# A decoder layer with attention, retention and a two-expert feed-forward: the experts' rows are added to one row per token in memory, the last norm loads all tokens at once, and the down products go chunk by chunk

## What is computed

```python
x = _layernorm(x + attention(x, Wq, Wk, Wv, Wo, bo))   # 16 heads of width 8, over the other rows of a token group
x = _layernorm(x + retention(x, ctx, ctx))             # decaying causal scores against ctx
router = x @ gate                                      # 8 experts, the best two per token, softmax over the two
hid = silu(x @ w1[e]) * (x @ w3[e])                    # 128 -> 512
x = _layernorm(x + sum over the two e of weight[e] * (hid @ w2[e]))
```

## Time and profile before

| | |
|---|---|
| device time, median of 3 runs | 1015.67 us (1014.71 to 1018.06) |
| profiled execution, first to last instruction (span) | 1027.0 us |
| PE busy, share of the span | 839.8 us, 82% |
| DVE | 794.7 us, 77% |
| POOL | 654.8 us, 64% |
| ACT | 607.7 us, 59% |
| mean granted TensorE clock | 0.914 of full speed |
| DMA | 72.72 MB, 71 GB/s over the span |

### The profile page before, as it was taken

The page is one execution under the profiler, slowest core; times in us unless marked ns, Lnnn a source line. Parts: engine busy times, 40 slices in busy tenths (PEclk is TensorE's granted clock), DMA queues, the critical chain, the costliest instruction groups (busy, mean ns, idle before and its releaser), DMA issues.

```text
span 1027.0 us, 35115 instructions
## 1 busy us (share of the span) xinstructions
PE 839.8 (82%) x12164; PEld 639.6 (62%) x12164; DVE 794.7 (77%) x2219; ACT 607.7 (59%) x1416; POOL 654.8 (64%) x738
## 2 busy tenths in 40 slices
PE   1667699999999999989979770699999999999600
PEld 1445466666666666656655440599899999999500
DVE  4787899998988989878856642588888888888575
ACT  1123457667667777666766851466666666666355
POOL 0338776699989999988997456044444444444443
PEclk9687899999999999999998965799999999999855
DMA  9312122122232231212222002222222222222186
GB/s 307 79 27 48 35 52 54 36 66 67 47 72 52 65 68 50 65 37 60 47 50 63 23 22 63 66 64 61 61 63 65 65 62 64 63 61 59 45 257 222
DMA packets 145303, 72.72 MB, mean 71 GB/s; under 512 B 75024, under 2 KB 134544, under 8 KB 145136
## 3 DMA queue, kind: packets, MB, share of 16 engines
q1 hardware_dynamic: 124800, 40.56, 17.1%
q0 software_dynamic: 8640, 17.84, 5.2%
q10 hardware_dynamic: 11696, 12.08, 3.6%
HBM read 42.11 MB, written 28.34 MB: 69 GB/s over the span
## 4 chain that ended last, share of the span: by engine, by line
PE 33%; POOL 28%; issue 11%; DVE 3%; DMA 2%; another core or an unknown queue 1%; ACT 1%; POOLq 0%; SPq 0%; DVEq 0%; ACTq 0%
POOL prod_ev L1551 14%; POOL routed_rows L1568 9%; PE QKV L773 9%; PE ST L773 9%; PE XT L801 5%; PE SC L801 5%; POOL rs L1531 3%; DMA prod_ev<-token_halves 1%; DMA routed_rows<-xe,pos 1%; PE YY L589 1%; POOL frs L1613 1%; PE YY L791 1%; PE TR L791 1%; PE SC L562 1%
## 5 line engine op out<-in xcount | busy, mean ns | idle before, releaser
L1551 POOL TENSOR_TENSOR prod_ev<-e_sb,q_v 128x512 f32<-128x512 f32 x256 | 300.3, 1206 | 77.5 <-PE YY L589 40.1
L1600 POOL DMA_INDIRECT token_halves<-w_new,tok_i x142 | 137.9, 971 | 32.5 <-issue 22.2
L1568 POOL DMA_INDIRECT routed_rows<-xe,pos x128 | 131.2, 1025 | 30.4 <-issue 30.0
L1151 DVE TENSOR_TENSOR prod_qk<-q_v,QKV 128x2048 f32<-128x2048 f32 x64 | 145.4, 2274 | 4.9 <-ACT q_v L870 4.9
L1453 DVE TENSOR_TENSOR prod_ev<-prod_qk,prod_ev 128x1024 f16<-128x1024 f32 x71 | 87.0, 1225 | 56.1 <-ACT prod_ev L1028 31.1
L773 PE MATMUL QKV<-k_t,w_hl 128*128 128x256 f16 x852 | 117.2, 274 | 0.0
L773 PE MATMUL ST<-k_t,w_hl 128*128 128x256 f16 x852 | 116.9, 274 | 0.0
L411 POOL TENSOR_TENSOR marks<-half_c 128x1 f32<-128x1 f32 x103 | 19.7, 192 | 149.7 <-DVE w_new L1469 149.1
L1037 ACT ACTIVATE prod_qk<-QKV,silu_scale 128x512 f32<-128x512 f32 x142 | 90.0, 683 | 41.3 <-PE QKV L773 41.3
L1028 ACT CAST prod_ev<-prod_qk 128x1024 f16<-128x1024 f32 x71 | 74.2, 1045 | 62.9 <-DVE prod_qk L1479 62.9
L1479 DVE SCALAR_TENSOR_TENSOR prod_qk<-ST,hid_scale,prod_qk 128x512 f32<-128x512 f32 x142 | 99.5, 742 | 2.9 <-PE ST L773 1.8
(11 more groups left out here) (171 smaller groups left out, 1785.9 us busy)
## 6 DMA issues: line engine op xcount, KB each, us to landing
w_new<-routed_rows SPq DMA_DIRECT2D x71, 130.0 KB
prod_ev<-token_halves SPq DMA_DIRECT2D x16, 512.0 KB, 4.9
x_sb<-x SPq DMA_DIRECT2D x32, 128.0 KB, 2.8
x_res<-x SPq DMA_DIRECT2D x128, 32.0 KB
head_rows<-o_n SPq DMA_DIRECT2D x32, 128.0 KB
o_t<-head_rows SPq DMA_DIRECT2D x64, 64.0 KB
ctx_sb<-ctx SPq DMA_DIRECT2D x32, 128.0 KB
out<-prod_qk ACTq DMA_DIRECT2D x16, 256.0 KB, 4.0
```

The source lines that it names most:

```text
L1151: eng.tensor_tensor(prod_qk[:, u, :, :].rearrange("p d (i j) -> p d i j", j=NH), q.unsqueeze(3).to_broadcast([P, HD, NH, NH]), k.unsqueeze ...
L1551: ins = eng.tensor_tensor(prod_ev[:, u, q, :, :, 0:HD], e_sb[:, it.slot(2), u, 64 * q:64 * q + 64].rearrange("p (i j) -> p j i", j=4).unsq ...
L1568: eng.indirect_dma_start(out=xs, out_offset=bass.IndirectOffsetOnAxis(ap=pos[:, r, 2 * u + k:2 * u + k + 1], axis=0), in_=xe[:, r, u, k, : ...
L1600: eng.indirect_dma_start(out=halves, out_offset=bass.IndirectOffsetOnAxis(ap=tok_i[:, s, u:u + 1], axis=0), in_=yw[:, s, u, :], in_offset= ...
```

## The change

Stage A also writes the normed x of each token, once, to a new tensor `token_sums` with one row per token: four direct DMAs a duo on SP's queue, behind the loads of `o_t` (`ROWS_LAG`). The row numbers behind the routed rows now name tokens, not halves. In stage B, `xh` and its half of x are gone, `yw` is the weighted product alone (`tensor_scalar`), and the indirect DMAs add their rows to `token_sums` (`compute_op`); since two tiles can hold the same token, POOL waits before each tile until the DMAs of the tile before have landed. The down products keep their matmuls and change their order. In stage C eight loads of 512 KB bring all sums at once into the memory of the weights `w1_hl` and `w3_hl`; there is no add of halves, ACT writes in place, and SP issues the stores. `C_FIRST` equals the number of chunks, so the stage is written out without a loop.

```diff
-        "spare_ids": 2 * n_tok + p[:, None] + P * np.arange(4 * n_exp)[None, :],
-        "ids": 2 * (P * b + row)[:, None] + 4 * P * (ids // 4) + 2 * S * (ids // 2 % 2) + ids % 2,
+        "spare_ids": n_tok + p[:, None] + P * np.arange(4 * n_exp)[None, :],
+        "ids": (P * b + row)[:, None] + 2 * P * (ids // 4) + S * (ids // 2 % 2),
...
-    PE_LAGS, ACT_LAGS, DVE_LAGS, POOL_LAGS, SP_LAGS = 13, 13, 14, 11, 9
-    CTX_LAG, HEADS_LAG = 9, 8
+    PE_LAGS, ACT_LAGS, DVE_LAGS, POOL_LAGS, SP_LAGS = 13, 13, 14, 11, 14
+    CTX_LAG, HEADS_LAG, ROWS_LAG = 9, 8, 14
...
-    C_FIRST, C_LAGS = 8, 3
+    C_FIRST, C_LAGS = n_chunks_c, 3
...
-    halves = nc.dram_tensor("token_halves", [2 * n_tok + 2 * n_exp * TILE, P], F32).ap()
+    sums = nc.dram_tensor("token_sums", [n_tok + 2 * n_exp * TILE, P], F32).ap()
...
-    half_rows = halves[0:2 * n_tok, :].rearrange("(p n k) d -> p n k d", p=P, k=2)
+    sum_duos = sums[0:n_tok, :].rearrange("(n u b h g) d -> n u b g h d", u=2, b=2, h=NH, g=4)
+    sum_rows = sums[0:n_tok, :].rearrange("(p n) d -> p n d", p=P)
...
-        fin = stage_b2[:, 0:RING * C_SLICES * 2 * P].rearrange("p (r n k d) -> p r n k d", r=RING, n=C_SLICES, k=2)
-        fout = stage_b[:, 0:RING * C_SLICES * P].rearrange("p (r n d) -> p r n d", r=RING, n=C_SLICES)
+        in_weights = [w[:, :, :].rearrange("p k w -> p (k w)").bitcast(F32).rearrange("p (c n d) -> p c n d", n=C_SLICES, d=P)
+                      for w in (w1_hl, w3_hl)]
+
+        def final_rows(c):
+
+            n = c.number()
+            return in_weights[n * 2 // n_chunks_c][:, n % (n_chunks_c // 2), :, :]
...
+                if it := at(ROWS_LAG):
+
+                    r = it.slot(RING)
+                    wait(it, x2_ready)
+                    for u in range(2):
+                        for b in range(2):
+                            eng.dma_start(sum_duos[it.number()][u][b], xe[S * u:S * u + S, r, b, 0, 0:P]).then_inc(rows_out[r], 16)
...
-                    wait(t, xh_ready, RING)
...
-
-                    wait(c, fout_ready, RING)
-                    eng.dma_start(fin[:, c.slot(RING), :, :, :],
-                                  half_rows[:, bass.ds(c.number() * C_SLICES, C_SLICES), :, :]).then_inc(fin_in[c.slot(RING)], 16)
-
-            run_steps(eng, n_chunks_c, C_FIRST, 0, last_norm)
+                    n, m = c.number(), n_chunks_c // 4
+                    eng.dma_start(in_weights[n // m][:, 2 * (n % m):2 * (n % m) + 2, :, :],
+                                  sum_rows[:, 2 * C_SLICES * n:2 * C_SLICES * (n + 1), :].rearrange("p (c n) d -> p c n d", c=2)
+                                  ).then_inc(fin_in[n], 16)
+
+            run_steps(eng, n_chunks_c // 2, C_FIRST // 2, 0, last_norm)
+
+            def store(at):
+                if c := at(0):
+                    wait(c, fout_ready)
+                    eng.dma_start(out_rows[:, bass.ds(c.number() * C_SLICES, C_SLICES), :], final_rows(c)).then_inc(fin_out, 16)
+
+            run_steps(eng, n_chunks_c, C_FIRST, 0, store)
+            eng.wait_ge(fin_out, 16 * n_chunks_c)
...
-                    for u in range(2):
-                        for n in range(n_chunk):
-                            cols = bass.ds(down_no * inner + P * n, P)
-                            for k, (h, wp) in enumerate(((hid_hi, 0), (hid_lo, 0), (hid_hi, 1))):
-                                mm = eng.matmul(YB[down.slot(2)][:, P * u:P * u + P],
-                                                h[:, down.slot(2), TILE * n + P * u:TILE * n + P * u + P], w2_hl[:, wp, cols],
-                                                start=(n == 0 and k == 0), stop=(n == n_chunk - 1 and k == 2))
+                    for n in range(n_chunk):
+                        cols = bass.ds(down_no * inner + P * n, P)
+                        for wp, terms in ((0, (hid_hi, hid_lo)), (1, (hid_hi,))):
+                            for u in range(2):
+                                for h in terms:
+                                    mm = eng.matmul(YB[down.slot(2)][:, P * u:P * u + P],
+                                                    h[:, down.slot(2), TILE * n + P * u:TILE * n + P * u + P], w2_hl[:, wp, cols],
+                                                    start=(n == 0 and wp == 0 and u == 0 and h is hid_hi),
+                                                    stop=(n == n_chunk - 1 and wp == 1), skip_group_check=True)
...
+                wait_ring(it, rows_out, RING, 64)
...
-                    wait_ring(t, xg_in)
-                    wait(t, yw_ready, RING)
-                    eng.mul(xh[:, t.slot(RING), :, :], xg[:, t.slot(RING), :, 0:P], 0.5).then_inc(xh_ready, 1)
...
-                    s, r = c.slot(2), c.slot(RING)
+                    y = final_rows(c)
                     wait(c, fnb_ready)
-                    wait_ring(c, fin_out, RING)
                     for n in range(C_SLICES):
-                        ins = eng.activation(fout[:, r, n, :], fin[:, r, n, 0, :], ACT.Identity,
-                                             bias=fnb[:, s, n:n + 1], scale=frs[:, s, n:n + 1])
+                        ins = eng.activation(y[:, n, :], y[:, n, :], ACT.Identity,
+                                             bias=fnb[:, c.slot(2), n:n + 1], scale=frs[:, c.slot(2), n:n + 1])
                     ins.then_inc(fout_ready, 1)
-                if c := at(3):
-                    wait(c, fout_ready)
-                    eng.dma_start(out_rows[:, bass.ds(c.number() * C_SLICES, C_SLICES), :],
-                                  fout[:, c.slot(RING), :, :]).then_inc(fin_out[c.slot(RING)], 16)
 
             run_steps(eng, n_chunks_c, C_FIRST, C_LAGS, last_norm)
...
-                    wait(t, xh_ready)
                     wait(t, wt_ready)
                     wait_ring(t, half_out, RING, 32)
                     for u in range(2):
-                        ins = eng.scalar_tensor_tensor(out=yw[:, s, u, :], in0=YB[t.slot(2)][:, P * u:P * u + P],
-                                                       scalar=wt[:, s, u:u + 1], in1=xh[:, s, u, :], op0=ALU.mult, op1=ALU.add)
+                        ins = eng.tensor_scalar(yw[:, s, u, :], YB[t.slot(2)][:, P * u:P * u + P], wt[:, s, u:u + 1], None, ALU.mult)
...
-                    y = fin[:, c.slot(RING), :, :, :]
-                    wait_ring(c, fin_in)
-                    eng.tensor_tensor(y[:, :, 0, :], y[:, :, 0, :], y[:, :, 1, :], ALU.add).then_inc(fsum_ready, 1)
-                    wait(c, fsum_ready)
+                    eng.wait_ge(fin_in[c.number() // 2], 16)
                     wait(c, fmv_ready, 2)
                     for n in range(C_SLICES):
-                        ins = eng.bn_stats(fstat[:, s, n, :], fin[:, c.slot(RING), n, 0, :])
+                        ins = eng.bn_stats(fstat[:, s, n, :], final_rows(c)[:, n, :])
...
+            for r in range(RING):
+                eng.wait_ge(rows_out[r], 64 * n_duo // RING)
...
+                    wait_ring(t, half_out, 1, 32)
                     stand(t, 5)
                     for u in range(2):
-                        eng.indirect_dma_start(out=halves, out_offset=bass.IndirectOffsetOnAxis(ap=tok_i[:, s, u:u + 1], axis=0),
-                                               in_=yw[:, s, u, :], in_offset=None).then_inc(half_out[s], 16)
+                        eng.indirect_dma_start(out=sums, out_offset=bass.IndirectOffsetOnAxis(ap=tok_i[:, s, u:u + 1], axis=0),
+                                               in_=yw[:, s, u, :], in_offset=None, compute_op=ALU.add).then_inc(half_out[s], 16)
```

More of the change, by code:

```diff
@@ L314, in in_new @@
             return w_new[:, at * RING * 2:(at + c) * RING * 2].rearrange("p (r u c) -> p r u c", r=RING, u=2)
-        xg, yw, xh = in_new(0, ROW), in_new(ROW, P), in_new(ROW + P, P)
+        xg, yw = in_new(0, ROW), in_new(ROW, P)
         x_hl = k_t[:, 0:2, :, :].rearrange("p r u t -> p (r u t)").bitcast(F16).rearrange("p (s k t) -> p s k t", s=2, k=2)
@@ L391, in build @@
             [sem(f"{n}{half}") for half in range(2)] for n in ("g_done", "u_done", "sil_ready", "hid_ready"))
-        xhi_ready, xlo_ready, xh_ready, hhi_ready, hlo_ready = (
-            sem(n) for n in ("xhi_ready", "xlo_ready", "xh_ready", "hhi_ready", "hlo_ready"))
+        xhi_ready, xlo_ready, hhi_ready, hlo_ready = (
+            sem(n) for n in ("xhi_ready", "xlo_ready", "hhi_ready", "hlo_ready"))
         yw_ready, tok_ready, wt_ready = (sem(n) for n in ("yw_ready", "tok_ready", "wt_ready"))
-        fin_in, fin_out = ring_sem("fin_in"), ring_sem("fin_out")
+        fin_in, fin_out = [sem(f"fin_in{n}") for n in range(n_chunks_c // 2)], sem("fin_out")
+        rows_out = ring_sem("rows_out")
         fnb_ready = sem("fnb_ready")
-        fsum_ready, fstat_ready, fmv_ready, fve_ready, frs_ready, fout_ready = (
-            sem(n) for n in ("fsum_ready", "fstat_ready", "fmv_ready", "fve_ready", "frs_ready", "fout_ready"))
+        fstat_ready, fmv_ready, fve_ready, frs_ready, fout_ready = (
```

(14 more changed lines are left out.)

## The result

The changed kernel is slower: 1130.17 us in the median of 4 runs (1127.57 to 1132.91) beside 1016.87 us for the kernel before on the same chip (4 runs, 1014.71 to 1019.43), a ratio of 1.1115 with a 95% interval of 1.108 to 1.1149. That is 113.3 us more, where 12.7 us less was forecast; 1062 us was the upper end of the range. The profiled execution took 1132.91 us; its span is 1131.1 us. The two pages can't be compared by their spans: stage A of the profiled execution of the kernel before took some 5 to 15 us longer than in the other profiles here (its first scatter of stage B stands at 664.95 us, in the changed kernel at 655.73, in the others between 650 and 660), so B and C are compared each by itself.

A forecast was written before the change was run, and what follows sets the result against it. The prediction took the DVE/ACT loop, 4.37 us a tile, to bound stage B. C's -14.3 us and +1.6 us at B's tail gave -12.7 us, so 1003.0 us from 1015.67; range 994 to 1062 us.

The forecast's parts named there:

- the plain chain of 3.94 us: Stage B, POOL: marks to second issue 1.63, landing 2.22, wake-up 0.09; under the 4.37 us pace, 0.43 us of slack.
- x: Stage B: all that adding adds to the scatter chain per tile; taken as 0.3 us, bounds 0 and 2.0.
- the first rival: Wait ahead of marks: scatter chain becomes B's bound, slower from x = 0.60; 1044 us at x = 1.0; slower chance 0.37.
- An issue's time on POOL follows its count of 128 rows, which stays.: Stage B scatters: argument for a small x, that adding leaves the issue's time on POOL unchanged.
- twice the descriptor work: Stage B scatters: alternative upper bound for x, 2 x 0.97 us.
- Fetching from HBM in place of SBUF is worth tenths: Stage B scatters: quickest HBM load and store both land in 2.0 us, so fetching old rows costs only tenths.
- The form of the sum: Whole kernel: net change -14.3 + 0.96 + 2x + 70 (x - 0.43), the last where positive; zero at x = 0.60.
- C: -14.3 us: Stage C: loads at once and no add cut the period to 1.92 us a chunk; sixteenth fnb at 1008.3, not 1022.59.
- B's pace by DVE and ACT: Stage B: the DVE/ACT loop of 4.37 us a tile sets the pace; PE fits in beside it.
- `yw` 0: Stage B, DVE: yw without the add saves 0, as it still reads PSUM; up to 0.077 us each otherwise.
- reorder 0: Stage B, PE: new down-product order frees up to 0.26 us a tile, hidden by the DVE/ACT loop, so 0.
- A 0: Stage A, SP: 128 more DMAs covered by SP's wait for o_n, so 0; without cover 32 x 2.3 = 73 us.

The follow-up runs named there:

- two tensors: Changed kernel with two sums tensors used by turns, POOL waiting for the tile two before, the two sums not brought together: 1004.06 us, ratio 0.9891.
- run with C at once: Kernel before with stage C's 16 loads issued all at once into the weight buffers, add of halves kept, stores on SP: 1008.20 us, ratio 0.9938.

## Why the prediction was wrong

**The step that failed** is the chain of POOL in stage B, in both of its terms: the plain chain of 3.94 us, which was to leave 0.43 us of slack, and x, "what adding costs", taken as 0.3 us between bounds of 0 and 2.0. That the scatter chain becomes the bound was the first rival, at 0.37, and its place, the wait ahead of `marks`, is where the runs show it. Three arguments made the chain too short:

- *The plain chain.* The landing of 2.22 us came from one row at the end of B; over B, in the run with the wait alone, it is 2.2 at the least, 2.3 in the median, 4.3 at the most. Also some 0.3 us between an open wait for a landing and the issue were missing. The quick loop is 4.41 us, over the 4.37 that were to hide it, so nothing is left to take up a late landing: in the mean it is 4.83, 33 us in the end. The slack of 0.43 us was not there at all.
- *"An issue's time on POOL follows its count of 128 rows, which stays."* The same 128 rows take 1.56 us in place of 0.96 to 0.98, and half of them hardly less. Twice a tile that is 1.2 us. The prediction's other upper bound, "twice the descriptor work" of 0.97 us, was the nearer thought; the runs show 0.6 us of it for each issue.
- *"Fetching from HBM in place of SBUF is worth tenths".* The part behind the issue did grow by tenths, though by more than the 0.3 taken for all of x: behind the second issue's end the next `marks` stands 3.62 - 1.56 = 2.06 us in the changed kernel (854.70 to 858.32) and 2.45 - 0.96 = 1.49 us with plain writes, 0.57 us more in these turns. Whether the fetch of the old rows makes it, no run shows.

Together, by quick turns: 3.94 forecast for plain writes; 4.41 with the wait; 6.12 with adding. So x itself measured 1.71, inside its bounds and far from 0.3, and the plain loop adds 0.47 that the prediction did not have; as one term that is 2.18, over the upper bound. By the means over B (4.83 and 6.14) the adding is worth 1.3 us a tile and the wait alone 0.46. With adding fewer turns are late, 8 of 70 at least 0.3 us over the median of 6.06, against 23 with plain writes; why, no run shows. The form of the sum held. With 2.18 for x it gives -14.3 + 0.96 + 4.36 + 70 x (2.18 - 0.43) = +113.5 us; measured were +113.3. By the traces B with its last landing is 127.1 us longer (126.0 from first to last scatter, and 1.1 more from the last issue to SP's first load) and C 13.8 shorter, 113.3 in all. The Trainium skill ("DMA: Bandwidth & Descriptors", Anatomy of one DMA) calls the time to generate descriptors small and variable, and puts most of a DMA's fixed time in the receipt of the write. Here the issue on POOL is not small, 0.96 us of the 2.3 from issue to landing with plain writes and 1.56 of 3.3 with adding; how the rest divides, no row shows.

**C: -14.3 us** was right: 1.93 us a chunk for 1.92 and 13.8 us less in all, and with B back at 4.37 us (two tensors) the kernel is at 0.9891 of before, 11 us faster, where the formula without the loss, 1002.3 us, is a ratio of 0.987, inside the interval. The run with C at once shows the half of it that comes from the late loads.

**B's pace by DVE and ACT, `yw` 0, reorder 0, A 0** were right: with two tensors `marks` stand 4.37 us apart with the new `yw` and the new order of PE; a `yw` instruction takes 343 ns in the mean before and with the new form; the order alone changes nothing; SP's wait covers the rows. The tail of B was too small with x: the last two tiles' `marks` stand 6.11 us apart in place of 2.98 (1079.07, 1085.18), and SP's first load comes 3.44 us behind the last issue in place of 2.36, +4.2 us where 1.6 was forecast.

**The chances.** The range went to x = 1.25, because equal landing times of loads and stores were taken to speak for a small x. They speak of the transfer, and not of the time that an issue holds POOL, which no row of the kernel before shows for an adding DMA; for that part the upper bound should have carried far more weight.

## What to carry to other kernels

A wait for one's own last DMA turns a latency that was hidden four slots deep into a loop: issue times, landing and wake-up add up once a turn. Compare that sum with the stage's pace by the median and the worst landing of the stage, not by one row: here a quick loop of 4.41 us against a pace of 4.37 cost 33 us, most of it by late landings. A wait one tile further back, with two sums tensors by turns, cost B nothing that shows; with one tensor two neighbouring tiles may hold the same token and the wait can't be moved. And take apart a change whose parts lie in different stages: with B back at its pace the change was worth 1.1%, nearly all of it in C, and that gain stood under a loss of 12% in B.

## What the hardware did that was not expected

An adding indirect DMA of 128 rows of 512 bytes holds POOL for 1.56 us, a plain one for 0.96 to 0.98, and both change little when the rows are halved (1.42 and 0.90). The queue of these DMAs (packets, MB, share of 16 engines' span), with adding in the changed kernel and plain with the wait kept:

```profile
q0 software_dynamic: 24544, 17.84, 11.7%
```
```profile
q0 software_dynamic: 8640, 17.84, 5.2%
```

The same bytes go in 15,904 packets more. 142 scatters with 128 packets each in place of 16 make just that difference, 142 x 112 = 15,904, and the sizes of the packets in the traces agree: 18,176 of 512 bytes with adding, one for each row, and 2,272 of 4096 bytes with plain writes, sixteen for each DMA. A plain DMA of 64 rows still has sixteen, of 2048 bytes.

That the longer issue comes from the number of packets is not shown, and the half rows speak against it for the larger part: an adding DMA of 64 rows has 64 packets fewer and is only 0.14 us shorter, so 112 more packets are worth an estimated 0.25 us at most (0.14 x 112 / 64), less than half of the 0.6. What the rest of it is, what makes single landings late, up to 4.3 us with plain writes, and what the 0.3 us behind an open wait for a landing are, stays open.
